# A residual kept at twice its value, and ScalarE's gate openings in two parts, in a four-layer sequence kernel

## The reference

```python
x = x + _L0_cond_ref(x, cond_1024[:, None, :], ...)   # causal convolution of 16 taps, 64 states, a linear scan over time
x = x + _L1_cond_ref(x, cond_1024, Wx, Wh, b)         # LSTM with 512 units, 512 steps, h0 = cond
x = x + _L2_cond_ref(x, itok, cond_1024, maa_k, maa_r, w_recept, w_key, w_value)
x = x + _L3_cond_ref(x, cond_1024)
```

```python
xprev = jnp.concatenate([shift_state[:, None, :], x[:, :-1]], axis=1)
xk = x + (xprev - x) * time_maa_k
xr = x + (xprev - x) * time_maa_r
```

```python
ax = jnp.abs(x)
p = ax / jnp.sum(ax, axis=1, keepdims=True)
pi = jnp.exp(p * TEMPERATURE)
cum = jnp.cumsum(pi / jnp.sum(pi, axis=1, keepdims=True), axis=1) + 0.001
chosen_idx = jnp.sum(cum <= rv, axis=1, keepdims=True)
gathered = jnp.take_along_axis(ax, chosen_idx, axis=1)
return x * (ax >= gathered)
```

## Time and profile before

| | us |
|---|---|
| median of 3 runs | 4191.82 |
| lowest and highest | 4191.44, 4198.04 |
| the profiled execution | 4197.63 |
| its span, first to last instruction | 4194.9 |
| TensorE busy in the span | 3890.3 (93%) |
| VectorE busy | 3109.5 (74%) |
| ScalarE busy | 1679.4 (40%) |
| GpSimd busy | 289.2 (7%) |

### The profile page before, as it was taken

The page is one execution under the profiler, slowest core; times in us unless marked ns, Lnnn a source line. Parts: engine busy times, 40 slices in busy tenths (PEclk is TensorE's granted clock), DMA queues, the critical chain, the costliest instruction groups (busy, mean ns, idle before and its releaser), DMA issues. The chain is left out here.

```text
span 4194.9 us, 112126 instructions
## 1 busy us (share of the span) xinstructions
PE 3890.3 (93%) x44034; PEld 2542.4 (61%) x44034; DVE 3109.5 (74%) x10143; ACT 1679.4 (40%) x5296; POOL 289.2 (7%) x410
## 2 busy tenths in 40 slices
PE   3999999999999999999999999999599999996885
PEld 3566666666656666665666666665277888783332
DVE  9888888888878888887888888865455544544887
ACT  3334333334333333433333443333244434443554
POOL 2000000000000000000000000000000000002433
PEclk8999999999999999999999999999899999998887
DMA  7111111111111111111111111101233343324432
GB/s 282 27 37 27 27 34 27 34 37 27 27 35 27 32 34 31 27 34 27 27 32 38 27 27 34 22 17 20 79 148 121 139 158 122 120 83 148 148 133 71
DMA packets 388634, 266.97 MB, mean 64 GB/s; under 512 B 289721, under 2 KB 323001, under 8 KB 385060
## 3 DMA queue, kind: packets, MB, share of 16 engines
q1 hardware_dynamic: 366416, 184.21, 16.4%
q0 software_dynamic: 17696, 66.79, 4.2%
q10 hardware_dynamic: 4020, 9.10, 0.6%
HBM read 176.48 MB, written 83.92 MB: 62 GB/s over the span
## 5 line engine op out<-in xcount | busy, mean ns | idle before, releaser
L387 PE MATMUL bank<-buf,buf 128*16 128x256 f32 x32768 | 1874.2, 380 | 67.0 <-DVE buf L704 57.8
L387 PEld LDWEIGHTS bank<-buf,buf 128*16 128x16 f32 x32768 | 906.0, 97 | 890.8 <-DVE buf L704 88.9
L837 PE MATMUL bank<-buf,buf 128*128 128x256 f32 (+1 forms) x3072 | 1037.1, 338 | 4.0 <-DVE buf L1008 2.7
L838 PE MATMUL bank<-buf,buf 128*128 128x256 f32 (+1 forms) x3072 | 979.0, 319 | 0.0
L839 PE MATMUL bank<-buf,buf 128*128 128x256 f32 (+1 forms) x3072 | 978.4, 318 | 0.0
L597 DVE SCALAR_TENSOR_TENSOR buf<-buf,buf,buf 128x256 f32<-128x256 f32 x1920 | 870.9, 481 | 3.2 <-issue 3.2
L682 DVE STREAM_TRANSPOSE buf<-bank 128x256 f32<-128x256 f32 x1024 | 459.4, 449 | 421.7 <-PE bank L387 386.8
L554 ACT ACTIVATE buf<-buf 128x96 f32<-128x96 f32 x1024 | 290.5, 284 | 1146.5 <-DVE buf L687 1146.0
L837 PEld LDWEIGHTS bank<-buf,buf 128*128 128x128 f32 x3072 | 582.0, 189 | 254.6 <-issue 216.3
L839 PEld LDWEIGHTS bank<-buf,buf 128*128 128x128 f32 x3072 | 583.9, 190 | 41.2
L838 PEld LDWEIGHTS bank<-buf,buf 128*128 128x128 f32 x3072 | 584.7, 190 | 38.5
(11 more groups left out here) (137 smaller groups left out, 2977.4 us busy)
## 6 DMA issues: line engine op xcount, KB each, us to landing
buf<-in_wk SPq DMA_DIRECT2D x16, 2048.0 KB, 9.5
buf<-in_wv SPq DMA_DIRECT2D x16, 2048.0 KB, 9.3
buf<-in_xT SPq DMA_DIRECT2D x62, 496.0 KB, 3.8
buf<-in_xT SPq DMA_DIRECT2D x32, 512.0 KB, 3.6
expert_in_scratch<-buf POOLq DMA_DIRECT2D x16, 1024.0 KB, 22.7
x_scratch<-buf SPq DMA_DIRECT2D x32, 512.0 KB, 9.2
buf<-expert_in_scratch SPq DMA_DIRECT2D x16, 1024.0 KB, 11.5
expert_out_scratch<-buf POOLq DMA_DIRECT2D x64, 256.0 KB, 4.7
```

The costliest lines, as they stand in the source:

```text
L387: last = mm(gate_ps[hf][32 * j:32 * j + B, 0:HCOLS], hist[:, k, at_step(slot_at)], wh[:, k, j * GCOLS + hf * HCOLS:j * GCOLS + (hf + 1) * ...
L837: nc.tensor.matmul(out, left[0], right[0], start=first, stop=False)
L838: nc.tensor.matmul(out, left[0], right[1], start=False, stop=False)
```

## The change

The residual in `stream`, in `x2_scratch` and in the finish stage's ring is twice the residual of before. For this the first layer's output weights are doubled, `center` is doubled as it is added, the shares of the mix are halved, the halo is doubled, and the input products are halved where they are taken out of their bank. `keep_x2` then adds `hist` as it is, in one operation over all four blocks; `combine` adds the gated rows as they are; `keep` yields 0.5 or 1. `center` is loaded from a second copy of the input, `xB`, which is ordered by tile, batch and time. In the finish stage ScalarE opens two gates of batch `i+2` ahead of the sides and two after the absolute values, and does the first exponent ahead of the gates of batch 1. SyncE loads the small vector `maa_r` first, on a semaphore of its own, and the residual of batches 3 to 5 only after batches 0 to 2 have been weighed. Of GpSimd's instructions the diff changes the halo's copies, which become multiplications by two.

```diff
-                sp.dma_start(center, x_dram[:, :, bass.ds(m * LTILE, LTILE)]).then_inc(s["center_landed"], 16)
+                sp.dma_start(center, ins["xB"][:, :, bass.ds(m * LTILE, LTILE)]).then_inc(s["center_landed"], 16)
...
-                v.tensor_tensor(stream[four][:, two(q), :, 1:], out_ps[q].rearrange("p (k b t) -> p k b t", k=2, b=B),
-                                center[:, two(q), :].rearrange("p k (t b) -> p k b t", b=B),
-                                ALU.add).then_inc(s["x1_ready"], 1)
+                v.scalar_tensor_tensor(out=stream[four][:, two(q), :, 1:].rearrange("p k b t -> p (k b) t"),
+                                       in0=center[:, two(q), :].rearrange("p k (b t) -> p (k b) t", b=B), scalar=2.0,
+                                       in1=out_ps[q].rearrange("p (n t) -> p n t", t=LSTEPS), op0=ALU.mult,
+                                       op1=ALU.add).then_inc(s["x1_ready"], 1)
...
-                for k in range(KD):
-                    kept = stream[four][:, k, :, 8 * u + 1:8 * u + 9]
-                    last = v.scalar_tensor_tensor(
-                        out=kept, in0=hist[:, k, u * P:(u + 1) * P].rearrange("p (t b) -> p b t", b=B), scalar=0.5,
-                        in1=kept, op0=ALU.mult, op1=ALU.add)
-                    last.then_inc(s["x2_done"], 1)
+                kept = stream[four][:, :, :, 8 * u + 1:8 * u + 9]
+                v.tensor_tensor(kept, hist[:, :, u * P:(u + 1) * P].rearrange("p k (t b) -> p k b t", b=B), kept,
+                                ALU.add).then_inc(s["x2_done"], 1)
...
+            v.tensor_scalar(maa_last, maa_k, 0.5, None, ALU.mult).then_inc(s["share_ready"], 1)
...
+            sp.dma_start(maa_r, ins["maa_r"]).then_inc(s["maa_landed"], 16)
             load(0)
-            sp.dma_start(maa_r, ins["maa_r"]).then_inc(s["weights_landed"], 16)
             sp.dma_start(wr, ins["wr"]).then_inc(s["weights_landed"], 16)
             for i in range(1, RING):
+                if i >= 3:
+                    sp.wait_ge(s["weighed"], KD * (i - 2))
                 load(i)
...
-                g.tensor_copy(stream[i % RING][:, :, 0:1], cond[:, :, i:i + 1]).then_inc(s["halo_ready"], 1)
+                g.tensor_scalar(stream[i % RING][:, :, 0:1], cond[:, :, i:i + 1], 2.0, None,
+                                ALU.mult).then_inc(s["halo_ready"], 1)
...
-            open_gate(0)
+            open_gate(0, 0, KD)
             weigh_last(2)
             absolute(0)
-            open_gate(1)
             exponent(0)
+            open_gate(1, 0, KD)
             weigh_last(3)
             for i in range(B):
+                if i + 2 < B:
+                    open_gate(i + 2, 0, 2)
                 take_sides(i)
                 if i + 1 < B:
                     absolute(i + 1)
                 if i + 2 < B:
-                    open_gate(i + 2)
+                    open_gate(i + 2, 2, KD)
                 if i + 1 < B:
                     exponent(i + 1)
...
-                    v.scalar_tensor_tensor(out=x2_of(i, k), in0=gated[k % 2], scalar=0.5, in1=x2_of(i, k),
-                                           op0=ALU.mult, op1=ALU.add).then_inc(s["x3_ready"], 1)
+                    v.tensor_tensor(x2_of(i, k), gated[k % 2], x2_of(i, k), ALU.add).then_inc(s["x3_ready"], 1)
...
-                    v.tensor_scalar(factor[k], ax[i % 2][:, k, 0:T], column(level, i, k), 1.0, ALU.is_ge,
-                                    ALU.add).then_inc(s["factor_ready"], 1)
+                    v.tensor_scalar(factor[k], ax[i % 2][:, k, 0:T], column(level, i, k), 0.5, ALU.is_ge,
+                                    ALU.max).then_inc(s["factor_ready"], 1)
```

More of the change, by code:

```diff
@@ L233, in tile @@
                 if later(n, 1):
-                    sp.wait_ge(s["x2_done"], 2 * KD * n)
+                    sp.wait_ge(s["x2_done"], 2 * n)
                     sp.sem_inc(s["sp_passed"], 1)
@@ L246, in _ @@
             tiles(sp, tile)
[L247 removed]
+            sp.wait_ge(s["x2_done"], 2 * NLT)
             sp.dma_start(x2_d.rearrange("p c b t -> p (c b) t")[:, :, (NLT - 1) * LSTEPS:],
@@ L491, in keep_inputs @@
                 a(xw[par][:, :, q, :], xw_ps[q % 2][:, 0:LTILE].rearrange("p (b t) -> p t b", b=B), ACT.Identity,
-                  bias=bias[:, q:q + 1]).then_inc(s["xw_ready"], 1)
+                  bias=bias[:, q:q + 1], scale=0.5).then_inc(s["xw_ready"], 1)
             def weigh_last(m, four, u):
@@ L497, in weigh_last @@
                     act.wait_ge(s["rows_turned"], r)
+                if not later(m, 1):
+                    act.wait_ge(s["share_ready"], 2)
                 act.wait_ge(s["halo_ready"], m + 1)
-                act.wait_ge(s["x2_done"], KD * (r + 1))
+                act.wait_ge(s["x2_done"], r + 1)
                 for k in range(KD):
                     a(mix[:, k, :].rearrange("p (b t) -> p b t", b=B), stream[four][:, k, :, 8 * u:8 * u + 8],
-                      ACT.Copy, scale=maa_k[:, k:k + 1])\
+                      ACT.Copy, scale=maa_last[:, k:k + 1])\
                         .then_inc(s["weighed"], 1)
@@ L521, in _ @@
             a(y_high[N_STATE:], ones[N_STATE:], ACT.Copy).then_inc(s["y_ones"], 1)
-            a(wo_pair, wo, ACT.Copy).then_inc(s["wo_high"], 1)
-            a(wo_rest[N_STATE:], bo_rows[N_STATE:], ACT.Copy).then_inc(s["wo_high"], 1)
+            a(wo_pair, wo, ACT.Copy, scale=2.0).then_inc(s["wo_high"], 1)
+            a(wo_rest[N_STATE:], bo_rows[N_STATE:], ACT.Copy, scale=2.0).then_inc(s["wo_high"], 1)
             for i, src in enumerate((dt_log, a_log)):
@@ L671, in mix_in @@
             def mix_in(m, four, u):
-                dve.wait_ge(s["share_ready"], 1)
+                if not later(m, 1):
+                    dve.wait_ge(s["share_ready"], 2)
                 for k in range(KD):
@@ L745, in _ @@
             dve.wait_ge(s["wo_high"], 2)
[L746 to L749, removed]
+            v.scalar_tensor_tensor(out=wo_rest[0:N_STATE], in0=wo[0:N_STATE], scalar=2.0,
+                                   in1=wo_pair[0:N_STATE].bitcast(F32), op0=ALU.mult,
+                                   op1=ALU.subtract).then_inc(s["wo_ready"], 1)
+            v.scalar_tensor_tensor(out=wo_rest[BO_LOW:OUT_ROWS], in0=bo_rows[BO_LOW:OUT_ROWS], scalar=2.0,
+                                   in1=wo_rest[BO_LOW:OUT_ROWS].bitcast(F32), op0=ALU.mult,
+                                   op1=ALU.subtract).then_inc(s["wo_ready"], 1)
             dve.wait_ge(s["cond_landed"], 16)
@@ L1039, in finish_phase @@
     wr = carve(KD, D)
-    maa_r, maa_now = carve(KD), carve(KD)
+    maa_r, maa_last, maa_now = carve(KD), carve(KD), carve(KD)
     stream = [carve(KD, 1 + T) for _ in range(RING)]
@@ L1156, in turn @@
                     last.then_inc(s["turned"], 1)
-            pe.wait_ge(s["weights_landed"], 32)
+            pe.wait_ge(s["weights_landed"], 16)
             receptance(0)
@@ L1179, in weigh_last, with open_gate @@
                         act.wait_ge(s["xr_ready"], KD * (i - 1) + k + 1)
-                    a(weighed[:, k, :], stream[i % RING][:, k, 0:T], ACT.Copy, scale=maa_r[:, k:k + 1])\
+                    a(weighed[:, k, :], stream[i % RING][:, k, 0:T], ACT.Copy, scale=maa_last[:, k:k + 1])\
                         .then_inc(s["weighed"], 1)
-            def open_gate(i):
-                for m in range(KD):
+            def open_gate(i, first, last):
+                for m in range(first, last):
                     act.wait_ge(s["r_summed"], KD * i + m + 1)
@@ L1352 @@
         "xT": spread(a["x"].transpose(2, 1, 0)).reshape(KD, P, NTOK),
+        "xB": spread(_np.swapaxes(a["x"].transpose(2, 0, 1).reshape(D, B, NLT, LSTEPS), 1, 2)).reshape(KD, P, NTOK),
         "ids": a["itok_BxS_2_50255"].reshape(P, NTOK // P),
@@ L1368 @@
            for k, v in arrays.items()}
-    ins["xT"] = ins["xT"].rearrange("c p n -> p c n")
+    for k in ("xT", "xB"):
+        ins[k] = ins[k].rearrange("c p n -> p c n")
     for k in ("condT", "Wh", "Wx", "Wp", "Ws", "wr", "wk", "wv"):
```

20 lines of the change are left out of this document (11 added, 9 removed).

## The result

The changed kernel takes 4145.18 us (median of 4 runs, 4144.85 to 4146.13), the kernel before 4193.68 us beside it (4 runs, 4191.44 to 4198.04): the ratio is 0.9883, 95% interval 0.9866 to 0.9901, so 48.5 us were won; 4144 were forecast. The profiled executions took 4144.85 and 4197.63 us, spans 4143.1 and 4194.9, so the two traces have 51.8 us to share out.

A forecast was written before the change was run, and what follows sets the result against it. TensorE bounds the recurrence; a loop of waits between TensorE and ScalarE holds the finish, and VectorE pays. Gains of 41 + 6 + 1 = 48 us take the median from 4191.8 to 4144 us, 8-in-10 range 4128 to 4164.

The forecast's parts named there:

- The finish: Finish stage: scan 15 moves from 4173.07 to 4132.1, so 41 us won.
- The mechanism: Finish rounds: TensorE's second half moves under sides and absolute values, the wait before the scan goes, rounds fall to 19.0 us.
- the floor: Finish round: VectorE's unbroken work from scans to the end of keep, 19.0 us, with nothing else coming later.
- The slow start: Finish, TensorE's blocks 2 and 3: 2.9 us extra after an idle at the lower clock, still ending under VectorE's work.
- The first round: Start of finish: scan 0 at 3835.1 instead of 3844.94, scan 1 at 3869.7.
- This lead is given back: First finish round: scan 0 comes 10 us earlier, yet scan 1 some 3 us later than before.
- the second place: First finish round: sides 0 stands behind gates 0 and 1 of batch 2, so sides end at 3857.7 plus 2.9.
- The new load order puts the small vector first, on a semaphore of its own: Finish start: first weighing no longer waits for the weights; TensorE starts at 3809.5 instead of 3812.27.
- The recurrence: Tile boundaries: merged addition takes 1.01 us for 1.20, 0.19 at each of 31 boundaries, 6 us (0 to 17).
- The addition at step 7 is under TensorE's work and gives nothing: Recurrence, step 7 of each tile: TensorE's work covers the merged addition, gain nothing; without cover 0.19 us a tile.
- The prologue: Before the loop: four cheaper block additions give 1.3 us, the added scale vector costs at most 0.2; 1 us.
- Rivals 1 and 2: First: GpSimd holds finish scans, 4180 us, chance 0.08; second: TensorE bounds the finish, 4179 (0.04) or 4274 us (0.04).

The follow-up runs named there:

- experiments 1 and 2: First: changed kernel, each batch's four gates opened in one run again, 4186.08 us; second: kernel before with only the new gate order, 4148.37 us.
- experiment 5: Changed kernel with gates 0 and 1 of batch 1 opened ahead of batch 0's exponentials, gates 2 and 3 behind them; 4137.78 us.
- Experiment 12: Changed kernel, GpSimd held until four factors made, batch 1's gates 0 and 1 before first exponentials, first-round sides and absolute values before batch 2's gates; 4111.58 us.
- experiment 9: Changed kernel with the residual addition at step 7 of each tile as four instructions, step 15 still as one; 4149.02 us.
- experiment 10: Kernel before with the input loaded in batch order, read straight by the addition of a block, as its only change; 4193.98 us.
- experiment 4: Kernel before with GpSimd's multiplication held until all four factors of a batch are made, as its only change; 4193.97 us.
- experiment 3: Changed kernel with GpSimd's multiplication held until all four factors of a batch are made, last batch block by block; 4120.66 us.

## Why the prediction was right

**The finish, 41 us forecast, 40.8 measured** (last scan 378.01 to 337.19 after the stage's start). The mechanism is the one named, by experiments 1 and 2: twelve rounds of 18.94 for 19.0, then 17.10 and 17.10 for 17.3 and 17.1, the scan at 4.54 with GpSimd beside it. One thing inside the floor was read as VectorE's own work and was not: 1.67 of the 19.0 us were VectorE waiting for GpSimd in the keep. It had stood in the kernel before, inside the same 3.34 us, and so cost the forecast nothing. The slow start, taken as 2.9 us in every round, came in six of the twelve rounds, where blocks 2 and 3 took 8.6 to 10.2 us instead of 7.1; it stayed under VectorE's work, as forecast.

**The first round.** Against the stage's start the first scan was forecast at 40.0 and came at 41.17, the second at 74.6 and 75.70; TensorE's products of batch 0 took 16.62 us for the 15.75 taken over from before. "This lead is given back" was right, and experiment 5 shows the first place that the prediction named, the gates of batch 1 behind the exponentials; the slow start taken there as 2.9 us was 3.0 (10.04 for 7.03). Experiment 12 moves the second place, the sides of batch 0 behind gates 0 and 1 of batch 2, together with the exponentials of batch 1: 5.9 us at the second scan. "The new load order puts the small vector first, on a semaphore of its own" joins two things: the semaphore gave 2.95 us at the first scan (2.8 forecast at TensorE's start), the order none.

**The recurrence, 6 us forecast, 8.6 between the traces.** At step 15 the merged addition took 1.03 us for the forecast 1.01, and 0.16 to 0.17 a tile came back for 0.19: 5 us. The mis-sized step is "The addition at step 7 is under TensorE's work and gives nothing": 0.07 to 0.11 a tile, 31 of them 2.2 to 3.4 us. The prediction shows no row of step 7 for this cover; the traces name TensorE as the releaser there, and experiment 9 shows that the transpose follows the addition. What the two steps leave of the 8.6 us, 0.2 to 1.4, is less than what a single span is uncertain by.

**The prologue, 1 us forecast, 1.4 between the traces** (first transpose 120.34 to 118.98); steps 11 and 12 gave nothing that the spans show. By experiment 10 the input in batch order alone has 0.6 us of it, within the 0.9 us by which the starts of the kernels with the old input differ. From the last transpose to the finish another 1.0 us went, which no part of the change was shown to cause.

**The sum.** The traces give 40.8 + 8.6 + 1.4 + 1.0 = 51.8, the forecast had 48. The medians lie 48.5 apart because the profiled execution of before was 4 us above its median and that of after was not; that the forecast of 4144 came nearer than its terms, which were 3.8 us short together, is luck. Rivals 1 and 2 did not come: the scan stayed at 4.54, and one pair of TensorE's blocks in four was slow, under cover.

## What to carry to other kernels

When two engines take turns waiting, move the instruction that frees the other's buffer ahead of work that nobody waits for yet, and then read what bounds the round next: an edit that is worth nothing while a wait absorbs it (experiment 4) can be worth half as much as the whole change once that wait is gone (experiment 3). Where four instructions of one form take 0.48 us and 1.31 us by turns, look at what runs beside them. A named releaser is a reading; whether an instruction has cover is settled by making it longer and looking whether the next one moves.

## What the hardware showed

The lock-step in the keep was the surprise: two of four factors took 1.3 us instead of 0.48 next to GpSimd's multiplication, while the scan was not touched. The other is TensorE's clock. In the changed kernel the pairs of blocks 2 and 3 start after an idle of about 3.2 us or after a shorter one, often by turns. Windows of three starts, the first and the second after 3.20 us, the third after 1.48; in the second the clock is at about the lower of its two levels (1.2 GHz), in the others at the higher (2.4 GHz):

```profile
3979.61:3982.80 3.19, 3.19 (x8) 1.52 (x9) 3.12 (x5) 3.19 (x10) 1.80 (x2) 1.00 1.02 392
...
3998.55:4001.74 3.19, 3.19 (x4) 1.40 (x5) 3.12 (x5) 3.19 (x10) 1.80 (x2) 0.53 1.03 394
...
4017.49:4020.68 3.19, 3.19 (x8) 1.51 (x9) 3.12 (x5) 3.19 (x10) 1.79 (x2) 1.00 1.04 401
```

The pairs take 7.13, 8.83 and 7.13 us. Of the seven pairs behind an idle of 2.8 to 3.2 us in these rounds six were slow (8.6 to 10.2 us) and one was not; what spared that one isn't shown. The five behind a shorter idle all took 7.13. In the rounds of 17.27 us of experiment 3 the idles are 1.2 to 1.5 us, every pair takes 7.03 or 7.13, and two whole rounds in a row have 1.00:

```profile
3976.00:3993.27 17.27, 15.76 (x51) 7.71 (x49) 17.06 (x33) 12.80 (x34) 9.12 (x9) 1.00 0.52 184
3993.27:4010.54 17.27, 15.74 (x50) 7.68 (x49) 17.06 (x33) 12.79 (x34) 9.10 (x9) 1.00 0.51 183
```

In the faster rounds TensorE stayed at its higher level, though nothing was done for that.
